# First unit projected straight onto its own partitions, stream loads spread over four units, six unread products ahead of the inputs

## The reference

```
result = (embeddings @ w_qkv).reshape(b, s, 3, 16, 8)        # q, k, v
scores = einsum('bnqd,bnkd->bnqk', q, k) / sqrt(128)
out    = einsum('bnqk,bnkd->bnqd', softmax(scores), v)
x = layernorm(x + out)
combine = top-8 of sigmoid(x @ gate_w.T) + expert_bias, weights normalised, times 2.826
y = sum_e combine_e * down_e(silu(gate_e(x)) * up_e(x)) + shared_down(silu(shared_gate(x)) * shared_up(x))
x = layernorm(x + y)
```

## Time and profile before

| | |
|---|---|
| median of 3 runs | 723.49 us (723.25 to 724.71) |
| the profiled execution, its own time | 725.11 us |
| its span in the profile | 723.4 us |
| mean granted TensorE clock | 0.966 of full speed |
| busy share of the span: PE, DVE, ACT, POOL | 95%, 71%, 57%, 44% |

### The profile page before, as it was taken

One profiled execution on the slowest core, in us unless ns is written; L12 is line 12 of the kernel. 1 busy time (PEld: TensorE's weight loads), 2 busy tenths in 40 slices (PEclk: granted clock), 3 DMA queues, 4 the chain that ended last, 5 costly groups with the idle time before them and its releaser, 6 DMA issues. The chain is left out here.

```text
span 723.4 us, 13286 instructions
## 1 busy us (share of the span) xinstructions
PE 687.6 (95%) x3494; PEld 361.9 (50%) x3494; DVE 515.3 (71%) x1085; ACT 415.6 (57%) x779; POOL 321.2 (44%) x371
## 2 busy tenths in 40 slices
PE   2899999999999999999997999999999999999995
PEld 1343333433434334343323767666676767676662
DVE  1889988999999999999953546557565655656343
ACT  2068877988879888787886424334343434334321
POOL 3033342423424252252230756665565646666563
PEclk8569999999999999999999999999999999999998
DMA  6832251422414233241105023050606032140600
GB/s 184 257 98 89 84 156 34 140 70 82 155 53 148 68 100 110 82 137 52 46 5 202 33 108 128 22 227 0 248 0 245 3 145 103 50 198 9 239 1 29
DMA packets 34279, 74.89 MB, mean 104 GB/s; under 512 B 4144, under 2 KB 13488, under 8 KB 30032
## 3 DMA queue, kind: packets, MB, share of 16 engines
q1 hardware_dynamic: 33440, 72.38, 29.1%
q0 software_dynamic: 816, 2.23, 1.1%
HBM read 58.61 MB, written 15.99 MB: 103 GB/s over the span
## 5 line engine op out<-in xcount | busy, mean ns | idle before, releaser
L743 ACT ACTIVATE probs<-ps_k 128x512 f32<-128x512 f32 x500 | 262.6, 605 | 51.7 <-PE ps_k L849 47.5
L786 DVE TENSOR_REDUCE maxima<-ps_bank 128x1 f32<-128x512 f32 x384 | 245.4, 682 | 27.5 <-PE ps_bank L842 22.4
L1085 POOL TENSOR_TENSOR hidden<-gated,weights 128x512 f32<-128x512 f32 x128 | 167.0, 1311 | 124.2 <-DVE gated L1167 108.4
L1115 ACT ACTIVATE silu<-ps_gate 128x512 f32<-128x512 f32 x136 | 81.3, 598 | 176.9 <-PE ps_gate L1209 176.6
L1167 DVE TENSOR_TENSOR gated<-silu,ps_up 128x512 f32<-128x512 f32 x128 | 87.0, 685 | 105.2 <-PE ps_up L1209 69.7
L842 PE MATMUL ps_bank<-k_aug,q_aug 32*128 32x512 f32 x384 | 147.9, 513 | 12.5 <-DMA q_aug<-q_rows 8.8
L849 PE MATMUL ps_k<-q_aug,k_aug 32*128 32x512 f32 x500 | 154.2, 489 | 4.0 <-ACT probs L743 2.2
L862 PE MATMUL ps_ctx<-probs,v_ones 128*32 128x512 f32 x1024 | 138.8, 614 | 0.9 <-ACT probs L743 0.9
L1234 PE MATMUL ps_y<-hidden,nets_down 128*128 128x512 f32 x272 | 137.1, 591 | 0.0
L849 PEld LDWEIGHTS ps_k<-q_aug,k_aug 32*128 32x128 f32 x500 | 64.0, 185 | 124.3 <-ACT probs L743 107.2
L1206 PE MATMUL ps_gate<-x1T_high,nets_low 128*128 128x512 f32 x136 | 96.5, 710 | 0.0
(11 more groups left out here) (117 smaller groups left out, 648.9 us busy)
## 6 DMA issues: line engine op xcount, KB each, us to landing
weights<-combine_rows SPq DMA_DIRECT2D x32, 1024.0 KB, 7.5
k_aug<-k_rows SPq DMA_DIRECT2D x32, 256.0 KB, 2.7
q_aug<-q_rows SPq DMA_DIRECT2D x32, 256.0 KB, 2.9
q_rows<-qk_high SPq DMA_DIRECT2D x16, 256.0 KB, 2.9
k_rows<-qk_high SPq DMA_DIRECT2D x16, 256.0 KB, 3.6
net_raw<-w_nets POOLq DMA_DIRECT2D x17, 128.0 KB, 2.4
xT_sb<-xT SPq DMA_DIRECT2D x8, 256.0 KB, 2.9
q_rows<-qk_low SPq DMA_DIRECT2D x8, 256.0 KB, 3.1
```

The costliest lines, as they stand in the source:

```text
L743: act.activation(probs[:, t, h, :], score_slot(i, last)[:], ACT.Exp, scale=ATT_SCALE).then_inc(exp_done, 1)
L786: dve.tensor_reduce(maxima[:, parity, TILES * h + t:TILES * h + t + 1], bank("q", (i - UNIT * AHEAD) % SCORES)[:], AX_X, ALU.max).then_inc ...
L1085: pool.tensor_tensor(hidden[:, s % RING, :], gated[:, s % UP_RING, :], r.weights[:, e, :], ALU.mult).then_inc(hidden_done, 1)
L1115: act.activation(silu[:, s % UP_RING, :], ps_gate[s % 2][:], ACT.Silu).then_inc(silu_done, 1)
```

## The change

The rows of unit 0 (heads 0 to 3 of batch 0) no longer go through DRAM. The host adds a weight matrix `w_unit` in which the q and k weights of these heads stand in the order of the 128 partitions of a slot, each head three times, with zeros for the pads. Two products with xT put q and k directly on their partitions. ACT rounds each to the high part, and DVE makes the rows with two operations: high times a sign per partition plus the pad value, then plus the product itself where the partition is a low row. The signs per partition come from the identity matrix by four small DVE operations ahead of the inputs. So `load_slot(0)` ahead of the body is gone, and unit 0 waits for DVE (`unit_rows`) and not for a DMA.

The ordinary projection of batch 0 follows behind those two products, into two banks of `ps_k`. ACT writes `qk_high` alone, and `first_qk_low` subtracts from PSUM; the one for k now stands behind the second maximum of unit 0.

The pads are made in slot 3. Six products of these pads (fp32r, all 128 partitions, 512 columns) run ahead of the wait for the inputs; nothing reads what they write.

The four `stream` loads move from ahead of the body into the units of batch 0, one behind each `spread_shift`. The three constant loads move to unit 0 of the last batch. GpSimd's wait for `stream` moves to where it first adds a context, in unit 3 of batch 0.

```diff
+    def first_unit(w):
+
+        rows = np.zeros((P, 2, GROUP, ROWS // HEAD, HEAD), w.dtype)
+        rows[:, :, :, :SHIFT_ROW // HEAD] = w.reshape(P, 3, HEADS, 1, HEAD)[:, :2, :GROUP]
+        return rows
...
+            def load_stream(part):
+
+                n = BATCHES * TILES // GROUPS
+                sp.dma_start(stream[:, part * n:(part + 1) * n, :], x_tiles[:, part * n:(part + 1) * n, :]
+                             ).then_inc(stream_loaded, DMA)
...
                     if not last or g < GROUPS - 1:
                         spread_shift(u + 1, (g + 1) % GROUPS)
+                    if first:
+                        load_stream(g)
+                    if last and g == 0:
+                        load_consts()
                     if g == 0 and not last:
...
             load_xT(0)
+            sp.dma_start(w_unit_sb[:].rearrange("p i d -> p (i d)"), w_unit).then_inc(w_unit_loaded, DMA)
             sp.dma_start(w_sb[:], w_qkv).then_inc(w_loaded, DMA)
...
-            load_slot(0)
             load_slot(1)
             load_slot(2)
-            for c in range(4):
-                n = BATCHES * TILES // 4
-                sp.dma_start(stream[:, c * n:(c + 1) * n, :], x_tiles[:, c * n:(c + 1) * n, :]
-                             ).then_inc(stream_loaded, DMA)
-            sp.dma_start(r.gate_w[:], gate_wT).then_inc(r.consts_loaded, DMA)
-            sp.dma_start(r.bias[:], expert_bias.unsqueeze(0).to_broadcast([P, EXPERTS])
-                         ).then_inc(r.consts_loaded, DMA)
-            sp.dma_start(nets_down[:].rearrange("p n d -> p (n d)"), w_downs).then_inc(r.downs_loaded, DMA)
...
                     if g == 3:
+                        if first:
+                            pool.wait_ge(stream_loaded, 4 * DMA)
                         add_context(pool, c, stream, 2 * b, b, 0)
...
+            def first_unit_high(i, src):
+                act.wait_ge(unit_projected, i + 1)
+                act.copy(unit_high[:, i, :], src[:]).then_inc(unit_highs, 1)
...
             def first_qk(i, src):
                 act.wait_ge(qk_projected, i + 1)
-                act.copy(qk_raw[:, i, :], src[:]).then_inc(qk_staged, 1)
                 act.copy(qk_high[:, i, :], src[:]).then_inc(qk_highs, 1)
...
+            def first_unit_rows(i, src, rows):
+
+                low = 1 + i
+                dve.wait_ge(unit_highs, i + 1)
+                dve.tensor_scalar(unit_part[:, i, :], unit_high[:, i, :].bitcast(F32), high_sign[:, low:low + 1],
+                                  pad_value[:, i:i + 1], ALU.mult, ALU.add).then_inc(unit_parts, 1)
+                dve.wait_ge(unit_parts, i + 1)
+                dve.scalar_tensor_tensor(rows[:, 0, :], src[:], row_kind[:, low:low + 1], unit_part[:, i, :],
+                                         ALU.mult, ALU.add).then_inc(unit_rows, 1)
...
+            dve.memset(k_aug[:, 3, :].bitcast(F32), -1.0).then_inc(pads_set, 1)
+            dve.memset(q_aug[:, 3, :].bitcast(F32), 0.0).then_inc(pads_set, 1)
+            take_row_kinds()
+            first_unit_rows(0, ps_bank[0], q_aug)
+            first_unit_rows(1, ps_bank[1], k_aug)
+            first_qk_low(0, ps_k[1])
             for u in range(AHEAD):
                 for i in range(UNIT):
                     take_maximum(u, 0, UNIT * u + i, u, False)
+                    if u == 0 and i == 1:
+                        first_qk_low(1, ps_k[2])
...
+            pe.wait_ge(pads_set, 2)
+            for n in range(6):
+                pe.matmul(ps_k[1 + n % 2][:], k_aug[:, 3, 0:P], q_aug[:, 3, :], start=True, stop=True)
             pe.wait_ge(xT_loaded, DMA)
+            pe.wait_ge(w_unit_loaded, DMA)
+            for i in range(2):
+                pe.matmul(ps_bank[i][:], w_unit_sb[:, i, :], xT_sb[:], start=True, stop=True
+                          ).then_inc(unit_projected, 1)
             pe.wait_ge(w_loaded, DMA)
...
             for u in range(AHEAD):
-                pe.wait_ge(slot_loaded[u], slot_loads(1))
+                if u == 0:
+                    pe.wait_ge(unit_rows, 2)
+                else:
+                    pe.wait_ge(slot_loaded[u], slot_loads(u, 1))
```

More of the change, by code:

```diff
@@ L144, in q_head_tile, with slot_loads, build @@
     return (i + 2) % GROUP, i // GROUP % TILES
-def slot_loads(times):
-    return DMA * 2 * times
-def build(nc, x, xT, w_qkv, w_nets, w_downs, gate_wT, expert_bias, out):
+def slot_loads(g, units):
+    return DMA * 2 * (units - (g == 0))
+def build(nc, x, xT, w_qkv, w_unit, w_nets, w_downs, gate_wT, expert_bias, out):
     q_rows = nc.dram_tensor("q_rows", [HEADS, ROWS, SEQ], F32).ap()
@@ L171, in build @@
         c = ContextState(nc, whole)
-        attention(nc, r, c, stream, nets_high, nets_low, nets_down, ident, x_tiles, xT, w_qkv,
+        attention(nc, r, c, stream, nets_high, nets_low, nets_down, ident, x_tiles, xT, w_qkv, w_unit,
                   w_nets, w_downs, gate_wT, expert_bias, q_rows, k_rows, shift_rows)
@@ L432, in load_weights, with attention @@
                  ).then_inc(r.weights_loaded[i], DMA)
-def attention(nc, r, c, stream, nets_high, nets_low, nets_down, ident, x_tiles, xT, w_qkv,
+def attention(nc, r, c, stream, nets_high, nets_low, nets_down, ident, x_tiles, xT, w_qkv, w_unit,
               w_nets, w_downs, gate_wT, expert_bias, q_rows, k_rows, shift_rows):
@@ L478, in attention @@
         w_loaded = sem("w_loaded")
+        w_unit_loaded = sem("w_unit_loaded")
+        row_kinds = sem("row_kinds")
+        row_signs = sem("row_signs")
+        unit_projected = sem("unit_projected")
+        unit_highs = sem("unit_highs")
+        unit_parts = sem("unit_parts")
+        unit_rows = sem("unit_rows")
         stream_loaded = sem("stream_loaded")
@@ L693, in _ @@
             load_net(0)
-            pool.wait_ge(stream_loaded, 4 * DMA)
             body(0, first=True)
@@ L793, in first_shift_low, with first_qk_low, take_row_kinds @@
                                   shift[:, 0, :].bitcast(F32), ALU.subtract).then_inc(shift_split, 1)
[L795 removed]
+            def first_qk_low(i, src):
                 dve.wait_ge(qk_highs, i + 1)
[L797 removed]
+                dve.tensor_tensor(qk_low[:, i, :], src[:], qk_high[:, i, :].bitcast(F32),
                                   ALU.subtract).then_inc(qk_split, 1)
+            def take_row_kinds():
+                dve.wait_ge(ident_set, 1)
+                dve.tensor_reduce(row_kind[:], ident[:].rearrange("p (h r d) -> p r h d", h=GROUP, r=ROWS // HEAD),
+                                  mybir.AxisListType.XY, ALU.add).then_inc(row_kinds, 1)
+                dve.wait_ge(row_kinds, 1)
+                dve.tensor_scalar(high_sign[:], row_kind[:], -2.0, 1.0, ALU.mult, ALU.add).then_inc(row_signs, 1)
+                dve.memset(pad_value[:, 0:1], 0.0).then_inc(row_signs, 1)
+                dve.tensor_scalar(pad_value[:, 1:2], row_kind[:, 3:4], -1.0, None, ALU.mult).then_inc(row_signs, 1)
+                dve.wait_ge(row_signs, 3)
+            def first_unit_rows(i, src, rows):
[6 more added lines that the diff above has]
+                                         ALU.mult, ALU.add).then_inc(unit_rows, 1)
             def body(b, first=False, last=False):
```

40 lines of the change are left out of this document (24 added, 16 removed).

## The result

| | before | after |
|---|---|---|
| median of 20 runs each | 726.07 us (722.54 to 733.36) | 718.53 us (715.37 to 723.55) |
| ratio after to before, 95% interval | | 0.9891 (0.9866 to 0.9915) |
| the profiled execution, its own time | 725.11 us | 716.71 us |
| its span | 723.4 us | 715.0 us |

By the ratio the change gains 7.9 us (6.2 to 9.7 by the interval); the two medians differ by 7.5.

A forecast was written before the change was run, and what follows sets the result against it. Bound: a start-up chain through DRAM leaving PE idle 8.8 us, then DVE until the body. Gain 6.4 - 0.7 - 0 - 0.3 = 5.4 us, set against the median: 718.1 us, range 714.3 to 721.3.

The forecast's parts named there:

- Term 1: Start of the kernel: the first maximum starts at 12.6 us instead of 19.02, a gain of 6.4 us.
- ahead of 5.5: Sign in the profile: the last unread product starts ahead of 5.5 us.
- Term 2: DVE in unit 0: the low part of k now stands behind the second maximum, costing 0.7 us.
- Term 3: Slot 1: its rows are there at 21.9 us and needed at 23.0, so the cost is 0.
- the sign that I had named for a wrong sum: Before the body: the sum is wrong if score_q of unit 1 waits for a DMA.
- Term 4: The four stream loads, moved into batch 0 among the row pieces, cost 0.3 us, between 0 and 3.0.
- Rival A: TensorE stays at full clock into the body, giving 714.0 to 717.1 us; chance 0.25.
- Rival B: The rows of batch 1 come late for unit 2, costing 3.0 us, so 721 us; chance 0.17.
- rival C: Slower: the clock's rise on batch 1's projections falls short; until the next projections, 729 us; chance 0.03.
- D: No change in time: slot 1 would have to come 5 us after the estimate; chance 0.03.
- The checks: Signs in the profile, among them first score_k about 32.1 us, unit 0's last maximum 22.3, unit 2 24 us after unit 0.

The follow-up runs named there:

- second pair: One more traced run each of the kernel before and the changed kernel, both unchanged: 726.19 us and 715.21 us.
- experiment 2: The changed kernel with the four stream loads and three constant loads put back ahead of the body: 720.38 us (12 runs), 0.9927 of the kernel before.
- experiment 4: The changed kernel with an unread plain f32 product of 128x128 behind each score_q of units 0 and 1: 740.12 us (6 runs), 1.0201 of before.
- experiments 1: The changed kernel without its six unread products: 718.11 us (6 runs), 0.9892 of the kernel before.
- 5: The changed kernel with three unread fp32r products in the other row groups from the ninth score_q on: 717.5 us (7 runs), 0.987 of before.
- 6: The changed kernel without the unread products and with the loads ahead of the body again: 720.45 us (12 runs), 0.9906 of the kernel before.
- 7: One more traced run of the changed kernel without the unread products and with the loads ahead of the body: 721.58 us.
- 8: The kernel before with only the stream and constant loads and GpSimd's wait moved: 725.9 us (12 runs), 0.999 of before.

## Why the prediction was right, point by point

The sign and the mechanism stood, and the size roughly: 5.4 us predicted at the head, 7.5 to 8.6 measured there and 7.5 between the medians. The 718.1 lies nearer to the 718.53 than it deserves, and that is luck: the gain was 2.1 us too small, and the base of three runs 2.6 us lower than the kernel's usual time. Two errors cancelled.

- **Term 1 was the term mis-sized**, 6.4 us where 8.1 was measured (19.02 - 10.96), and 9.2 in the second pair (19.15 - 9.93).
  - The unread products follow each other every 0.45 us (2.14 to 4.86 for six) and not every 0.59. They hold the inputs back by 0.46 us, not 1.2. The last starts at 4.4, as the check "ahead of 5.5" asks.
  - The price of a q or k product at full clock was the error in kind. I took 1.12 us from the earlier trace rows, which is the duration of a group of two records, so that the last one's latency is in it. When products follow each other, one takes 0.86 (q at 7.72 to the value products at 9.44 in the first trace after: 1.72 for two). It is a duration taken for a pitch, for three products: 0.8 us.
  - The clock was guessed to rise at 6.3 and rose near 7 in one trace and at about 5, just behind the start of unit 0's products, in the other two. The value products ended at 10.4, not 12.0.
  - PE binds, as said, in the first trace (0.28 us of wait in front of the maximum); in the second one DVE does. There the length of L842 counts: 0.55 us where a `tensor_tensor` takes 0.69. The Trainium skill, "VectorE: DVE Perf Modes", section "The perf-mode tier table", gives such an operation within SBUF twice the rate of a `tensor_tensor`, for 2048 elements. Carried over to the 512 here, that would be about half the time, an estimate; the trace shows a fifth less.
- **Term 2** was 0.7 and is 0.6: the maxima of unit 0 take 9.58 us from first to last start, for 8.98 in the earlier trace rows (19.02 to 28.00).
- **Term 3** was 0 and is 0. Slot 1's rows landed at 16.65 and its load held TensorE for 1.0 us near 20 (the row below). So the sign that I had named for a wrong sum, a `score_q` of unit 1 waiting for a DMA, was there in all three traces, and it cost nothing: DVE had `score_q` results waiting, and its maxima ran without a gap, 9.58 us busy of 9.58. The sign should have been an idle DVE. The slot was in use from 20.16, 1.8 us ahead of the transpose at 21.98, where I had given it 1.1.

```profile
20.13 0.28 PEld L894 LDWEIGHTS ps_bank<-k_aug,q_aug 32*128 32x128 f32 x1 [0.97 <-DMA q_aug<-q_rows]
```

- **Term 4** was 0.3 and is 0. A stream load takes SP 0.40 us here and not a quarter of 6.25. In the earlier trace rows four are issued in a row behind the slot loads; that the queue was full there is my reading and not shown. The rows of batch 1 followed at 39.38, 7.47 us earlier, exactly the head's gain. But the loads' place is worth some 5.3 us of the head once the maxima are early (experiment 2). The prediction asked only what the move costs, and not what the loads would block if they had stayed: the shift of unit 0 behind 3 MB of loads. Its sum came out right because the change moves both together.
- **Rival A** did not come: the granted clock was 0.50 at the first `score_k` in all three traces of the changed kernel. The Trainium skill, "TensorE: Matmul & The Clock Gate", section "Why this matters for your kernels", ties the fall to an idle gap. In experiment 4 it fell with no gap at all in the profile ahead of it, so here the measurement decides.
- **Rival B** did not come either: in batch 0 no `score_k` behind the first one waited for `q_aug<-shift_rows`, in any trace. In batch 1 one waited for 0.24 us in one of the changed kernel's three traces. There the wait came at length in the kernels of experiments 1 (1.7 us), 4 (1.6), 5 (2.5), 6 (1.6), 7 (1.2) and 8 (1.6), and in before in one trace of two. So it comes with the loads in either place; it was never the 512 KB in unit 0 of batch 0, and what decides on it is not shown.
- **Rivals C and D**: the clock rose on the projections of batch 1 in all three traces (at 48.1 inside the value products, which start at 47.60, and in the other two at 39.2 and 39.3 inside the k product), and the slot was on time. Two things in C were wrong all the same. In the earlier trace rows the clock rose at 49.6, 1.7 us behind the end of the k product of batch 1 (45.88 + 2.08 = 47.96) and ahead of its value products (52.88), not on them. And from 49.6 to 87.42 is 37.8 us, which at 0.35 costs 13 us and not 11, so 731 us and not 729.
- **The checks**: the first `score_k` was asked for at 32.1 and came at 30.36, 29.33 and 29.35, the last maximum of unit 0 at 22.3 and came at 20.54, and unit 2 24 us after unit 0: 26.7 in the first trace (57.09 - 30.36), 23.7 in the other two. In those, the clock rose near 39.2, 10 us into the body.

What remains is the difference between runs: over 161 runs of all these kernels, with a level for each kernel, the time rises by 0.38 us (0.35 to 0.41) for each us in which the clock is at its low level (span times twice what the mean granted clock lacks to 1.00), and 1.2 us of spread is left. The prediction's 0.35 for rival C was good.

## What to carry to other kernels

When a chain through DMA is cut at the start of a kernel, look at once at what stands in the queue ahead of the *next* small DMA on that chain: here the same change without the moved loads puts the shift behind loads of 3 MB, and the parts that give nothing clear of the noise alone (the loads, the unread products) give some 5.3 and about 1 us of the head once the chain is short. Price a series of products by its pitch, from start to start, and never by the duration of a group, which holds the last one's latency as well. Take the base from many runs where the spread is as large as the gain, and compare the runs' clocks before a gain is put down to a place.

## What the runs showed of the hardware

- TensorE's clock can fall under uninterrupted work: at 13.6 us in experiment 4, with PE busy, by the profile, for 2.50 of 2.50 us just ahead of it. This is one trace.
- The moment at which it rises differs from run to run for the same program: near 7 us or near 5 at the start, near 48.1 or 39.2 us in batch 0. With the first the body's start moved by 1.0 us, with the second the length of the first two units by 3.0 (26.7 for 23.7).
- A 16 KB DMA that was issued while some 1.5 MB of loads ahead of it were still to be moved took 6.6 us to the next step, for 1.4 with nothing ahead of it. The queue and the DMA engines are the same for both, so whether its place in the queue or the shared engines held it isn't told apart. Issuing a 512 KB load takes 0.40 us with no load ahead of it, and 1.4 on average when four are issued in a row behind the slot loads (5.46 us in experiment 2).
- `tensor_scalar` on 128x4 and 128x1 with scalars per partition took 1.13 and 1.05 us in the setup of the changed kernel, twice the 0.55 of one on 128x512. That is hardly their own cost: both end within 0.03 us of the end of GpSimd's `memset` of 2048 columns, in every trace of a kernel that has them, while the reduction L830 took 0.23 us beside the same `memset`. So `tensor_scalar` seems to have stood still until GpSimd was through; no run moves the `memset`, so this is not tested.

```profile
1.56 1.81 POOL L703 MEMSET v_ones<- 128x2048 f32 x1
...
2.00 0.23 DVE L830 TENSOR_REDUCE row_kind<-ident 128x4 f32<-128x128 f32 x1
...
2.26 1.13 DVE L833 TENSOR_SCALAR high_sign<-row_kind 128x4 f32<-128x4 f32 x1
...
2.35 1.05 DVE L835 TENSOR_SCALAR pad_value<-row_kind 128x1 f32<-128x1 f32 x1
```
